# How the parts of queries and keys reach DRAM and come back, in the first attention of a vision tower

## The reference, cut to what matters

```python
q = split_heads(tokens @ Wq, HEADS)
kv = split_heads(tokens @ Wkv, HEADS)
k, v = (kv[..., :DK], kv[..., DK:])
q, k, v = (l2norm(q), l2norm(k), l2norm(v))
sim = jnp.einsum('bhid,bhjd->bhij', q, k)
attn = jnp.square(jax.nn.relu(sim))
out = jnp.einsum('bhij,bhjd->bhid', attn, v)
out = tanh_norm(out)
```

## Time and profile before

| | |
|---|---|
| median of 3 runs | 3128.6 us (3127.97 to 3133.56) |
| the profiled execution's own time | 3139.85 us |
| its span in the profile | 3138.1 us |
| busy: TensorE, VectorE, ScalarE, GpSimd | 93%, 67%, 46%, 37% of the span |
| DMA, hardware queue (SP's) | 135138 packets, 187.50 MB, 23.9% of 16 engines |
| landing of `kparts<-kh`, `qparts<-qh` | 2.5 us, 2.4 us (median) |
| landing of `ks<-kparts`, `qs<-qparts` | 3.3 us, 3.8 us (median) |

### The profile page before, as it was taken

How to read it: one execution, slowest core, us unless ns; L and a number is a source line. 1 busy time by engine, 2 the same in 40 slices (tenths; PEclk the granted TensorE clock), 3 DMA queues, 4 the chain that set the end, 5 groups by cost and what they waited for, 6 DMA issues and landing times. The chain is left out here.

```text
span 3138.1 us, 66657 instructions
## 1 busy us (share of the span) xinstructions
PE 2907.1 (93%) x21548; PEld 2217.3 (71%) x21549; DVE 2098.8 (67%) x5372; ACT 1442.7 (46%) x2948; POOL 1157.0 (37%) x966
## 2 busy tenths in 40 slices
PE   3899999999999999999966999999999972999998
PEld 1677777777777777777744666666766652999997
DVE  4577677677677777777734777777777855444444
ACT  0444544545545545445422555555555533444443
POOL 3324434434434334334321233333233324444443
PEclk7899999999999999999987999999999985999999
DMA  3424424424424424324302111111111101554544
GB/s 83 96 70 92 107 66 95 107 62 98 102 62 104 98 66 104 94 70 104 87 22 51 49 47 53 43 42 52 45 54 47 44 33 44 77 76 76 77 77 69
DMA packets 161126, 223.12 MB, mean 71 GB/s; under 512 B 30305, under 2 KB 125730, under 8 KB 161074
## 3 DMA queue, kind: packets, MB, share of 16 engines
q1 hardware_dynamic: 135138, 187.50, 23.9%
q0 software_dynamic: 25936, 34.95, 7.2%
HBM read 125.26 MB, written 97.08 MB: 71 GB/s over the span
## 5 line engine op out<-in xcount | busy, mean ns | idle before, releaser
L66 POOL TENSOR_TENSOR vrn<-vsm,inv_root 128x16 f32<-128x16 f32 x64 | 243.8, 3809 | 285.8 <-DVE vsm L836 285.8
L665 ACT ACTIVATE R<-psA 128x1024 f32<-128x1024 f32 x256 | 262.4, 1025 | 168.4 <-PE psA L1150 164.2
L857 DVE TENSOR_TENSOR PR<-R 128x1024 f32<-128x1024 f32 x256 | 321.3, 1255 | 0.0
L2512 POOL DMA_INDIRECT out_rows<-e_y,e_dest x137 | 213.7, 1560 | 289.8 <-DMA out_rows<-e_y,e_dest 182.2
L1904 DVE TENSOR_REDUCE m_nm<-psC 128x4 f32<-128x1028 f32 (+1 forms) x256 | 239.0, 956 | 72.0 <-PE psC L2177 71.4
L1165 PE MATMUL psA<-PR,V 128*64 128x258 f32 x2048 | 283.4, 398 | 0.0
L670 ACT ACTIVATE oTs<-psA 128x258 f32<-128x258 f32 x256 | 99.1, 387 | 358.1 <-PE psA L1165 352.3
L1783 ACT ACTIVATE m_PT<-psC 128x770 f32<-128x770 f32 x256 | 194.0, 810 | 137.3 <-PE psC L2205 137.3
L1210 PE MATMUL psA<-wout,OT 128*128 128x256 f32 x1024 | 244.6, 382 | 0.4 <-DVE OT L899 0.4
L1698 POOL DMA_INDIRECT xg<-tn,idx x124 | 124.5, 1004 | 318.6 <-DMA xg<-tn,idx 186.6
L1210 PEld LDWEIGHTS psA<-wout,OT 128*128 128x128 f32 x1024 | 188.7, 191 | 24.6 <-DVE OT L899 0.7
(11 more groups left out here) (417 smaller groups left out, 7633.0 us busy)
## 6 DMA issues: line engine op xcount, KB each, us to landing
ks<-kparts SPq DMA_DIRECT2D x256, 128.0 KB, 3.3
qs<-qparts SPq DMA_DIRECT2D x256, 128.0 KB, 3.8
e_x<-xg SPq DMA_DIRECT2D x143, 129.0 KB
xraw<-in_x SPq DMA_DIRECT2D x66, 256.0 KB
qparts<-qh SPq DMA_DIRECT2D x128, 128.0 KB, 2.4
kparts<-kh SPq DMA_DIRECT2D x64, 128.0 KB, 2.5
kparts<-kl SPq DMA_DIRECT2D x64, 128.0 KB, 2.4
qparts<-ql SPq DMA_DIRECT2D x64, 128.0 KB, 2.4
```

Of the source, the lines that this page charges most:

```text
L66: return pool.tensor_tensor(out, x, e.to_broadcast(list(out.shape)), ALU.pow)
L665: act.activation(R[:, p % 2].rearrange("p a t n -> p t a n"), ps[:, 0:2, :].rearrange("p t (a n) -> p t a n", a=2), ACT.Relu).then_inc(rel ...
L857: dve.tensor_tensor(PR[:, p % 2, :, :, 0:L], R[:, p % 2], R[:, p % 2], ALU.mult).then_inc(prob_done, 1)
L2512: pool.indirect_dma_start(out, bass.IndirectOffsetOnAxis(ap=dest[:, b % XD:b % XD + 1], axis=0), y[:, b % XD], None, compute_op=ALU.add).t ...
```

## The change

The parts are written whole: one transfer for each of the five, `part[:]` with 2 KB contiguous in each of 128 partitions, to a DRAM tensor in which the two chunks of a row lie side by side. The high parts are written as soon as `k_sq` and `q_sq` have come; the second copy of `qh` goes before `ql`. The reads then pick every second 1 KB: 32 x 4 pieces of 1 KB each instead of 32 of 4 KB, through the function `heads`. The counts that are waited for are halved with the number of writes. The bytes are the same, and the computation too.

```diff
-            def keep_parts(tiles, rows, out):
-                for n, part in enumerate(tiles):
-                    for hh in range(2):
-                        sp.dma_start(rows[:, hh, n].rearrange("c x n -> x c n"),
-                                     part[64 * hh:64 * hh + 64].bitcast(F32)).then_inc(out, 16)
+            def keep_part(part, rows, n, out):
+                sp.dma_start(rows[:, n], part[:].bitcast(F32).rearrange("p c n -> p (c n)")).then_inc(out, 16)
+
+            def heads(rows, hh, n, c):
+                return rows[hh, n:n + 2].rearrange("a (r m) (c n) -> c (a r) m n", m=4, c=KT)[c]
...
-                        sp.dma_start(ks[to:to + 32, 4 * c:4 * c + 4].bitcast(F32).rearrange("p m n -> p (m n)"),
-                                     v.kparts[c, hh].rearrange("a (r m) n -> (a r) (m n)", m=4)).then_inc(moved, 16)
+                        sp.dma_start(ks[to:to + 32, 4 * c:4 * c + 4].bitcast(F32),
+                                     heads(v.kparts, hh, 0, c)).then_inc(moved, 16)
...
-                        sp.dma_start(qs[to:to + 32, hh, 4 * c:4 * c + 4].bitcast(F32).rearrange("p m n -> p (m n)"),
-                                     v.qparts[c, hh, n:n + 2].rearrange("a (r m) n -> (a r) (m n)",
-                                                                        m=4)).then_inc(moved, 16)
+                        sp.dma_start(qs[to:to + 32, hh, 4 * c:4 * c + 4].bitcast(F32),
+                                     heads(v.qparts, hh, n, c)).then_inc(moved, 16)
...
                 if c == 0:
+                    sp.wait_ge(k_sq, j + 1)
+                    keep_part(kh, v.kparts, 0, k_out)
                     sp.wait_ge(kl_done, j + 1)
-                    keep_parts((kh, kl), v.kparts, k_out)
+                    keep_part(kl, v.kparts, 1, k_out)
+                    sp.wait_ge(q_sq, j + 1)
+                    keep_part(qh, v.qparts, 0, q_out)
+                    keep_part(qh, v.qparts, 2, q_out)
                     sp.wait_ge(ql_done, j + 1)
-                    keep_parts((qh, ql, qh), v.qparts, q_out)
-                    sp.wait_ge(k_out, 64 * j + 64)
+                    keep_part(ql, v.qparts, 1, q_out)
+                    sp.wait_ge(k_out, 32 * j + 32)
                     lay_out_keys(0, moved0)
-                    sp.wait_ge(q_out, 96 * j + 96)
+                    sp.wait_ge(q_out, 48 * j + 48)
                     lay_out_queries(0, moved0)
...
-    v.kparts = nc.dram_tensor("kparts", (KT, 2, 2, P // 2, L), F32, kind="Internal").ap()
-    v.qparts = nc.dram_tensor("qparts", (KT, 2, 3, P // 2, L), F32, kind="Internal").ap()
+    v.kparts = nc.dram_tensor("kparts", (2, 2, P // 2, KT * L), F32, kind="Internal").ap()
+    v.qparts = nc.dram_tensor("qparts", (2, 3, P // 2, KT * L), F32, kind="Internal").ap()
```

## The result

| | median | lowest to highest | runs |
|---|---|---|---|
| before | 3128.28 us | 3125.87 to 3133.56 | 4 |
| with the change | 3790.57 us | 3789.17 to 3792.11 | 4 |

The ratio is 1.2114 [1.2093, 1.2135]: 662 us more. The prediction was 3830 us, in a range of 3660 to 4050; its forecast case came about, and what is left between is 39 us.

A forecast was written before the change was run, and what follows sets the result against it. TensorE, busy 2907.1 of 3138.1 us, was taken as the bound, with no margin for later transfers. Waits 633 plus clock 80 less 10 gave 703 us more, from the median 3128.6 us to 3830 us; range 3660 to 4050.

The forecast's parts named there:

- forecast case: The five writes run on the same two DMA engines, giving 3830 us; chance 0.85.
- What bounds the kernel: First attention: TensorE busy 1485.33 of 1500 us; transfers arrive with no margin, at most 0.3 us of delay absorbed.
- Two engines: The five part writes, with 2 outermost in DRAM, use 2 engines, the same two each time; reads stay on 16.
- cuts between outer rows: Transfers are dealt to DMA engines by cuts falling between outer rows on both sides; 2 outer rows allow only one.
- 87 ns a piece: Cost of a 2 KB piece in the new writes, from the `h2` store; five writes on two engines take 27.8 us.
- the prediction's other bound: 80 ns for each 2 KB piece of the new writes, an estimate for quiet neighbours: 25.6 us for five writes.
- The period grows by the whole delay: First attention: the similarity product starts 19.8 us later and each sample's period grows by all of it.
- The waits, 633 us: TensorE's added waits for the query transfers: 19.0 us in the first sample plus 31 x 19.8 us.
- The clock, 80 us: TensorE runs at half clock after each sample's wait, losing 2.5 us in each of 32 samples.
- 10 behind PR: Gain of 0.3 us per sample as the value product's wait for the probabilities PR no longer shows.
- The 51 us to the profiled execution: Forecast against the profiled execution: 3139.85 + 703 = 3843 us; the median of three runs lies 11 us lower.
- 703: Total time added by the change: 633 us of waits plus 80 us of clock, less 10 us.

The follow-up runs named there:

- experiment 5: Changed kernel with DRAM laid out so the five whole writes are 128x512 on both sides and each read is split in two: 3157.56 us, ratio 1.0068.
- experiment 4: Changed kernel with writes in halves of 64 rows, except both key parts whole (3372.72 us, ratio 1.0750) or only the high keys whole (3197.79 us, ratio 1.0195).
- experiments 1: Changed kernel with each whole write cut into two halves of 64 rows, 2 KB pieces and 1 KB gathers kept: 3131.76 us, ratio 1.0000.
- experiment 3: Changed kernel with writes in halves, each half cut into 57 + 7 rows (3522.39 us, ratio 1.1247) or 62 + 2 rows (3791.86 us, ratio 1.2118).

## Why the prediction was right

The prediction's steps, in its order:

- **What bounds the kernel.** Right. No margin between the transfers and TensorE, so each us of lateness is paid in each sample: experiment 5 shows it at 1 us, experiment 4 at 2 and 6, the changed kernel at 19.
- **Two engines.** Right in the count (small packets, a share of 0.13), and experiments 1 and 3 show it as the cause. The reason as the prediction gave it was incomplete: with "cuts between outer rows" alone, 62 rows would use 16 engines, and they use 2. The prediction set the rule of the Trainium skill (DMA: Bandwidth & Descriptors, "Why a DMA increments its semaphore by 16 and not by 1") beside its own as the same; it is another, and the one that the runs bear out: the number that divides the outer sizes decides. The trace of before held only sizes for which the two agree, so the step was right for a write with 2 outermost and would have failed for one with 62.
- **87 ns a piece.** Near: 85 ns on average, 80 once the writes run (the prediction's other bound), slower in the first four us. The row that it was taken from gives 88 (11.3 us / 128), a slip of 1 ns. The query reads are issued 28.5 us after the first write (934.13 - 905.59), where the steps give 29.1.
- **The period grows by the whole delay.** Right: 68.3 us against 47.3.
- **The waits, 633 us.** 608 were added. The product starts 33.5 us after the squares and not 34.2, nearly all of it because the query reads went out earlier; 32 x 0.7 is 22 of the 25 us.
- **The clock, 80 us, less 10 behind PR.** 54 in all instead of 70. After the restart the clock stands at half for 4.6 us, 2.3 us lost, where I took 2.5. From the product to the second product it is 6.57 us (939.07 to 945.64) where it was 4.44, and from there to the value product 0.65 instead of 0.86, since the wait behind PR no longer shows: 0.2 us a sample, or some 7 us, where I took 0.3 and 10. For this sample the busy time grew by 1.9 us (49.1 in a period, 47.2 before); 32 of these are 62. The 8 us that are missing to 54 fit what I left out, that some samples of before had lost time to the clock already (1.5 us behind the wait at 101.16, for one) and do not lose it twice; this part was not taken apart further.
- **The 51 us to the profiled execution.** 3843 was forecast for it and 3792 measured: 25 in the waits, 16 in the busy time, and 10 of idle time elsewhere, most of which has nothing to do with the change.
- **A detail that was wrong and cost nothing.** I had SP issue the key reads after two writes, at about 12.6 us from the first write. They came at 15.4, because SP was held in its issues; they hid all the same.

Together 608 + 54 = 662 stands against 703: the sum was 41 us too high, 25 in the waits and 16 in the busy time. Two things were luck: the 85 ns are the mean of a faster pace and a slow start, which I had not split, and a write with 2 outermost is a shape for which the prediction's rule and the right one agree.

## What to carry to other kernels

Before transfers are merged, compare the outermost sizes of both sides: the number of DMA engines is the largest up to 16 that divides both, and a merge that puts a 2 outermost turns 16 engines into 2, whatever the bytes and the pieces. Count the smallest packets in the profile: they give the number of engines per transfer at once. And one such transfer is not harmless because nothing needs it soon: every other transfer has a part of its pieces behind it on the busy engines, what waits for it holds up all that comes later in an in-order queue, and the issues of that queue can themselves be held up.

## What the runs showed of the hardware that was not expected

- **Issuing blocks when few engines hold the backlog.** An issue that takes 0.5 us took 4 to 5 us once about two whole writes were unfinished on the two engines (8.11 us for two, 5.45 for the next, in the changed kernel), and four halves took 5.01 instead of 2.53 us behind a single whole write. In experiment 3 the writes of 62 rows were held up too, 10.03 us for the eight of `qh`. With 16 engines (experiments 1 and 5) it did not show in the samples looked at. 5.4 us is about what one whole write takes on its two engines (64 x 85 ns, an estimate), as if each further issue had to wait until one write was through. How much may be outstanding before it begins was not measured by itself.
- **Issue times differ by shape, not by bytes.** A write of 128x512 that is one stride on both sides takes SP 0.32 to 0.45 us; with the 2 outermost 0.50 to 0.56 before any blocking; halves of 64x512 0.55 to 0.60, hardly less than the writes before, which were 64x2x256 (0.61 to 0.63). The reads of 32x4x256 take 0.60, those of 32x1024 before 0.42.
- **The clock's cost has little to do with how long the wait was.** Before, a wait of 3.55 us cost 1.5 us of half clock and one of 3.4 us cost 3.0. In the changed kernel a wait of 19 us costs mostly 2.2 (6.6 us from a product to the second instead of 4.44). With the keys whole (experiment 4), after waits of some 6 us, it is 1.3 in some samples and 2.9 in others.
